# The second half of a feed-forward layer in float16 pairs instead of float32, in a transformer block on one core

## The chip, the core and the metric

The kernel runs on 1 core of a Trainium2 chip. The core has five engines that run their own lists of instructions in order and meet at semaphores: TensorE (PE; matrix products, with PEld for its weight loads), VectorE (DVE), ScalarE (ACT), GpSimd (POOL) and SyncE (SP, which here only starts transfers). The metric is the device time of one execution in microseconds.

## The reference

One transformer block over x of shape (2, 512, 256), in float32: layer norms with per-batch scale, shift and gate computed from a vector c; attention with 32 heads over 8 key-value heads of width 64; and a mixture of experts in LoRA form, of which this case is about the second half.

```
logits = xf @ gate_w.T;  top_w, top_i = top_k(logits, 2);  routing = softmax(top_w)
base1 = xf @ w1.T;       base3 = xf @ w3.T                 # F = 704, E = 8 experts, R = 16
for each expert e with weight we:                          # zero but for the two chosen
    h1 = base1 + xf @ A1.T @ B1.T * 2;   h3 = base3 + xf @ A3.T @ B3.T * 2
    act = silu(h1) * h3
    acc += we * (act @ w2.T + act @ A2.T @ B2.T * 2)
x = x + gb * acc
```

## The kernel before

All arithmetic runs transposed: features on the 128 partitions, the 512 tokens of one batch along the free axis. A float32 product whose operands are split into a float16 high part and a float16 low part is done as three float16 matmuls (`mm3`: high x high, low x high, high x low). Attention and the feed-forward part's first half do that. A high part is a cast on ScalarE (`..._h`), a low part the difference of value and high part, on VectorE or GpSimd (`..._l`).

The attention part runs in 67 periods, n = -3 to 63, one head per period. Each engine's list is written out for the periods: TensorE transposes the probabilities of head n+1, multiplies those of head n with the values, and computes the scores of heads n+2 and n+3; ScalarE casts probabilities and takes exponentials; VectorE takes row maxima, subtracts, and normalises. Weights come in 30 chunks of 256 KB through four staging slots (`wst`), are cast by ScalarE (`w_h`) and differenced by GpSimd (`w_l`). In period 54 SP loads `a2` and `w2` in float32 into the space of used chunks (L340, L341).

The feed-forward part takes the two batches in turn (b = 0, 1), each in FT = 6 tiles of up to 128 of the 704 features (the sixth has 64), i = 6b + f. For each token only the two chosen experts matter. Masks of the routing (`maskT`) let one product serve both. TensorE, for tile f: `h_base` and `h_lora` of tile f+1 (12 + 6 float16 matmuls), `h_second` of tile f (6 more, which add the difference between second and first choice to the same banks), then `z_product`: the a2 product, in float32, of each choice s (L638). ScalarE takes the silu of h1 (`sil`, L888), VectorE multiplies by h3 (`pr`, L1195) and by the routing weight (`av`, L1202), and GpSimd adds both choices (`gsum`, L1363). After the sixth tile TensorE multiplies the sums with w2 and adds the b2 product of the masked LoRA sum `uT`, for four tiles of 128 tokens, in float32 (L700, L704). VectorE multiplies the result by the gate and adds it to x (`store_sum`, L1211, L1214), and SP stores it.

In the first batch's six tiles the three slower engines' lists also hold what the second batch needs: row statistics and norm (L913 to L945), modulation (`hT`, L818, L820), logits, first and second choice (L1110 to L1145), weights, masks (L863) and LoRA inputs (`tm`, L1162, L857, L1166).

What sets the order is the written list of each engine alone. There is no planner.

Of the kernel before, what the change touches and what calls it, by code (L numbers as in the profile page):

```python
# [8 lines left out]
F16 = mybir.dt.float16  # L9
# [35 lines left out]
N_CHUNKS = FFN_CHUNK + FFN_CHUNKS  # L45
WSLOTS = 4
# [51 lines left out]
def block_kernel(nc, x, chunks, cos, sin, cT, wmod, w2T, gateT, a2T, b2T, out, spill):  # L98
    ctx = ExitStack()
    with ctx:  # L100
# [16 lines left out]
        b2_sb = sb("b2_sb", [P, D])  # L117
# [53 lines left out]
        gsum = sb("gsum", [P, FT, S])  # L171
        uT = sb("uT", [P, 2, S])
        maskT1 = sb("maskT1", [P, 5, S])
        tm1 = sb("tm1", [P, 4, S])

# [19 lines left out]
        w2_sb = chunk_space(w_h, 0, [P, FT, D])  # L195
        a2_sb = chunk_space(w_l, 0, [P, FT, P])
# [6 lines left out]
        def ffn_cols(t, at, n):  # L203
# [5 lines left out]
                        for t in (w_h, w_l))  # L209
        maskT = (maskT0, maskT1)  # L210
# [3 lines left out]
        ld_x, ld_x1, ld_c, ld_mod, ld_mod2, ld_rope, ld_ffn, ld_w2 = (  # L214
            sem(f"ld_{k}") for k in ("x", "x1", "c", "mod", "mod2", "rope", "ffn", "w2"))
# [10 lines left out]
        wh_ready, wl_ready = sem("wh_ready"), sem("wl_ready")  # L226

# [17 lines left out]
            "h2h", "h2l", "h_mm", "silu", "p", "a", "g", "d_mm", "z_mm", "zm", "u", "o_mm", "og", "o")}  # L245
# [24 lines left out]
        def _(sp):  # L270
# [43 lines left out]
            sp.dma_start(b2_sb[:, :], b2T).then_inc(ld_ffn, 16)  # L314
# [9 lines left out]
            for n in range(FIRST_PERIOD, HEADS):  # L324
# [27 lines left out]
        def _(pe):  # L352
# [170 lines left out]
            for n in range(FIRST_PERIOD, HEADS):  # L523
# [893 lines left out]
```

## Time and profile before

| | |
|---|---|
| three runs, us | 547.51, 547.8, 545.5; median 547.51 |
| profiled execution: time, span | 547.47 us, 545.5 us |
| mean granted TensorE clock | 0.967 |
| PE busy (share of the span), instructions | 473.2 us (87%), 4424 |
| DVE, ACT, POOL busy | 364.1 (67%), 332.2 (61%), 275.2 us (50%) |
| chain that ended last, by engine | PE 65%, DVE 12%, ACT 11%, issue 7%, DMA 3% |
| L700, w2 product, and L638, a2 product, in that chain | 4%, 3% |

The span is the time between the first and last recorded instruction; the device time is 2.0 us longer. Matmuls are pipelined, so the record of one matmul (0.38 us for 512 float16 columns) is longer than the step to the next. A float32 matmul is recorded as two. In the page's line PEclk, one digit for each fortieth of the span, 9 is full clock; the slices at 450 and at 330 us are lower.

### The profile page before, as it was taken

The numbers are of one execution on the slowest core, as the hardware profiler recorded it, in microseconds if no ns is written. First come the engines' busy times: TensorE is split into PE (matmuls) and PEld (weight loads), VectorE is DVE, ScalarE is ACT, GpSimd is POOL, SyncE is SP. The second block draws the span as 40 slices with busy tenths as digits, with TensorE's granted clock in tenths as the row PEclk, the third lists the DMA queues.
The fourth block names the chain that finished last, engine by engine and source line by source line (L and its number), as shares of the span: only waits on it lengthen the run. The fifth ranks groups of instructions, "written<-read, shape, count | busy, mean of one in ns | idle before, by whom it ended". The sixth has DMA issues, their size and how long they took to land.

```text
span 545.5 us, 11950 instructions
## 1 busy us (share of the span) xinstructions
PE 473.2 (87%) x4424; PEld 324.4 (59%) x4424; DVE 364.1 (67%) x1022; ACT 332.2 (61%) x592; POOL 275.2 (50%) x202
## 2 busy tenths in 40 slices
PE   4777688889999999999999956889788979999997
PEld 3353556576676777777777735667654534464444
DVE  3674866778777778777788868887757766423342
ACT  3336579888878878888888874877624443101110
POOL 4345488885759876669999663310102313101110
PEclk9977889999999999999999996999999989999999
DMA  8046041585333564333545322251110000010001
GB/s 306 31 136 212 21 117 41 155 159 153 99 72 85 157 116 130 106 82 94 174 103 122 89 41 77 59 158 23 30 30 0 2 0 1 0 34 6 0 2 38
DMA packets 58169, 44.47 MB, mean 82 GB/s; under 512 B 36608, under 2 KB 50432, under 8 KB 58112
## 3 DMA queue, kind: packets, MB, share of 16 engines
q1 hardware_dynamic: 56624, 41.60, 29.5%
q10 hardware_dynamic: 1488, 2.10, 1.1%
q8 instruction: 36, 0.59, 0.5%
q14 instruction: 21, 0.17, 0.1%
HBM read 23.77 MB, written 11.53 MB: 65 GB/s over the span
## 4 chain that ended last, share of the span: by engine, by line
PE 65%; DVE 12%; ACT 11%; issue 7%; DMA 3%; POOL 1%; SPq 0%; ACTq 0%; DVEq 0%
PE ps L454 10%; PE ps L380 8%; PE ps L381 8%; PE ps L382 8%; ACT prob L763 6%; PE ps L700 4%; PE ps L472 4%; PE ps L436 4%; PE ps L476 4%; PE ps L438 4%; PE ps L474 4%; PE ps L638 3%; PE ps L628 3%; DVE pl L1044 2%; DMA spill<-rot 1%
## 5 line engine op out<-in xcount | busy, mean ns | idle before, releaser
L763 ACT ACTIVATE prob<-prob,least 128x512 f32<-128x512 f32 (+3 forms) x256 | 131.7, 551 | 3.1 <-DVE least L1036 3.1
L454 PE MATMUL ps<-ident,prob 128*128 128x128 f32 x640 | 95.2, 284 | 35.6 <-DVE pl L1044 19.7
L1036 DVE CUSTOM_DVE_ANT_0 prob<-ps,causal 128x512 f32<-128x512 f32 (+3 forms) x256 | 114.5, 485 | 11.9 <-PE ps L438 11.4
L770 ACT ACTIVATE ph<-ps 128x512 f16<-128x512 f32 (+1 forms) x128 | 89.5, 700 | 43.6 <-PE ps L454 40.1
L454 PEld LDWEIGHTS ps<-ident,prob 128*128 128x128 f32 x640 | 69.4, 143 | 50.5 <-DVE pl L1044 26.0
L1044 DVE SCALAR_TENSOR_TENSOR pl<-ps,ph 128x512 f16<-128x512 f32 (+1 forms) x128 | 99.1, 815 | 0.0
L436 PE MATMUL ps<-kT_h,qT 128*128 128x512 f16 (+3 forms) x256 | 77.3, 303 | 6.7 <-DMA qT<-spill 4.1
L1301 POOL TENSOR_TENSOR on_l<-on,on_h 128x512 f16<-128x512 f32 x32 | 37.1, 1161 | 87.2 <-ACT on_h L777 87.2
L438 PE MATMUL ps<-kT_l,qT 128*128 128x512 f16 (+3 forms) x256 | 70.7, 304 | 0.0
L472 PE MATMUL ps<-vh,ph 128*128 128x65 f16 x640 | 66.9, 197 | 0.6 <-DVE acc L1068 0.6
L474 PE MATMUL ps<-vl,ph 128*128 128x64 f16 x640 | 66.8, 196 | 0.0
L476 PE MATMUL ps<-vh,pl 128*128 128x65 f16 x640 | 66.7, 196 | 0.0
L472 PEld LDWEIGHTS ps<-vh,ph 128*128 128x128 f16 x640 | 60.2, 99 | 1.2 <-DVE pl L1044 0.9
L474 PEld LDWEIGHTS ps<-vl,ph 128*128 128x128 f16 x640 | 60.0, 100 | 0.6
L1053 DVE RECIPROCAL rsum<-ps 128x4 f32<-128x4 f32 x64 | 11.7, 183 | 72.4 <-PE ps L476 72.4
L476 PEld LDWEIGHTS ps<-vh,pl 128*128 128x128 f16 x640 | 59.9, 99 | 0.0
L380 PE MATMUL ps<-hT_h,w_h 128*128 128x512 f16 (+1 forms) x136 | 54.4, 400 | 5.8 <-DVE hT_l L965 2.9
L1363 POOL TENSOR_TENSOR gsum<-av 128x512 f32<-128x512 f32 (+1 forms) x12 | 15.2, 1264 | 86.1 <-DVE av L1202 86.1
L381 PE MATMUL ps<-hT_l,w_h 128*128 128x512 f16 (+1 forms) x136 | 54.4, 400 | 0.0
L382 PE MATMUL ps<-hT_h,w_l 128*128 128x512 f16 (+1 forms) x136 | 53.8, 395 | 0.0
L888 ACT ACTIVATE sil<-ps 128x512 f32<-128x512 f32 (+1 forms) x24 | 13.5, 594 | 65.6 <-PE ps L628 65.5
L1296 POOL TENSOR_TENSOR rot<-rot 128x1024 f16<-128x1024 f32 x19 | 40.6, 2137 | 16.4 <-ACT rot L742 16.3
(150 smaller groups left out, 957.2 us busy)
## 6 DMA issues: line engine op xcount, KB each, us to landing
spill<-rot SPq DMA_DIRECT2D x20, 512.0 KB, 3.6
qT<-spill SPq DMA_DIRECT2D x16, 512.0 KB, 3.5
wst<-chunks SPq DMA_DIRECT2D x30, 256.0 KB, 4.0
kT_h<-spill SPq DMA_DIRECT2D x8, 256.0 KB, 4.0
oT<-wmod ACTq DMA_DIRECT2D x3, 512.0 KB, 11.3
kT_l<-spill SPq DMA_DIRECT2D x4, 256.0 KB, 5.0
out<-xs SPq DMA_DIRECT2D x4, 256.0 KB, 2.1
w_h<-w2T SPq DMA_DIRECT2D x1, 640.0 KB, 5.1
```

What stands on the lines that cost most here:

```text
L380: pe.matmul(o, lh, rh, start=first, stop=False)
L381: pe.matmul(o, lh, rl, start=False, stop=False)
L382: return pe.matmul(o, ll, rh, start=False, stop=last)
L436: pe.matmul(ps[:, bank, off:off + w], qT[:, q_slot(u, j), c], kT_h[:, sg % 2, kv, 0:w], start=True, stop=False)
L438: mm = pe.matmul(ps[:, bank, off:off + w], qT[:, q_slot(u, j), c], kT_l[:, sg % 2, kv, 0:w], start=False, stop=True)
L454: mm = pe.transpose(ps[:, PT_BANK + c // 512, c % 512:c % 512 + P], prob[:, m % 2, c:c + P], ident[:, :])
L472: pe.matmul(ps[:, PV_BANK, at:at + HD + 1], ph[:, m % 2, c:c + P], vh[:, sg % 2, kt, kv, :], start=first, stop=False)
L474: pe.matmul(ps[:, PV_BANK, at:at + HD], ph[:, m % 2, c:c + P], vl[:, sg % 2, kt, kv, :], start=False, stop=False)
L476: mm = pe.matmul(ps[:, PV_BANK, at:at + HD + 1], pl[:, m % 2, c:c + P], vh[:, sg % 2, kt, kv, :], start=False, stop=last)
L763: act.activation(prob[:, m % 2, c], prob[:, m % 2, c], ACT.Exp, bias=least[:, m % 2, qt:qt + 1], scale=-1.0).then_inc(exp_done, 1)
L1036: ins = dve.tensor_tensor_reduce(prob[:, m % 2, at:at + w], ps[:, bank, off:off + w], causal[:, S - w:S], -1.0 / HD ** 0.5, 3.0e38, ALU.ad ...
L1044: dve.scalar_tensor_tensor(out=pl[:, m % 2, c], in0=ps[:, PT_BANK:PT_BANK + 3, :].rearrange("p a b -> p (a b)")[:, c], scalar=PROB_SCALE, ...
```

## The change

The a2, w2 and b2 products become three float16 matmuls each. For that `a2`, `w2` and `b2` are laid out as five more chunks of 256 KB. SP loads all five in period 54 into `raw` and `rot`, buffers of the attention part that are free by then; ScalarE casts one in each of periods 55 to 59, and GpSimd subtracts one in each of periods 56 to 60. The activations `av`, the sums `gsum` and the LoRA sum `uT` are split for each tile. The a2 products of a tile are issued one tile later; those of the sixth tile lie between two pieces of the w2 product; the b2 products of batch 0 come after the first tile of batch 1. The float32 `gsum` keeps two tiles instead of six. The steps that make the second batch's masks and LoRA inputs move one tile later. Cut to its core:

```
@@ kernel constants, SP, ScalarE
+LATE_CHUNKS = LATE_COLS // 512      # 5
+LATE_AT = 54
-                if n == 54:
-                    sp.wait_ge(proj_done, len(TILES))
...
+                if n == LATE_AT:
+                    lowered(sp, len(ITEMS) - 1)
+                    for i in range(LATE_CHUNKS):
+                        sp.dma_start(late_stage(i), chunks[N_CHUNKS + i]).then_inc(ld_late, 16)
+            def late_high(i):
+                act.wait_ge(ld_late, 16 * LATE_CHUNKS)
+                act.wait_ge(proj_done, len(TILES))
+                act.activation(w_h[:, i, :], late_stage(i), ACT.Copy).then_inc(late_h, 1)
@@ TensorE
-            def z_product(b, f, s):
-                pe.wait_ge(fs["a"], 2 * (b * FT + f) + s + 1)
-                mm = pe.matmul(ps[:, 4 + s, :], a2_sb[0:m, f, :], av[0:m, s, :], start=(f == 0), stop=(f == FT - 1))
+            def z_product(b, f):
+                for s in range(2):
+                    pe.wait_ge(fs["al"], 2 * i + s + 1)
+                    mm = mm3(ps[:, 4 + s, :], a2_h[0:m, f, :], a2_l[0:m, f, :], av_h[0:m, i % 2, s, :], av_l[0:m, i % 2, s, :],
+                             f == 0, f == FT - 1)
+            def b2_product(b, t):
+                pe.wait_ge(fs["ul"], b + 1)
+                for l, r in ((u_h, b2_h), (u_h, b2_l), (u_l, b2_h)):
...
                     h_second(b, f)
                     if f > 0:
-                        z_product(b, f - 1, 1)
-                    z_product(b, f, 0)
+                        z_product(b, f - 1)
+                    if b == 1 and f == 0:
+                        for t in range(T):
+                            b2_product(0, t)
...
+                for t in range(2):
+                    for f in range(FT - 1):
+                        w2_product(b, t, f)
+                z_product(b, FT - 1)
+                for t in range(2, T):
+                    for f in range(FT - 1):
+                        w2_product(b, t, f)
+                for t in range(T):
+                    w2_product(b, t, FT - 1)
+            for t in range(T):
+                b2_product(1, t)
@@ ScalarE, each tile
                         act.activation(sil[0:m, s, :], ps[0:m, bank, :], ACT.Silu).then_inc(fs["silu"], 1)
                         if b == 0 and f == 1 and s == 0:
                             modulate_ffn(1, 6)
+                        if i > 0 and s == 0:
+                            sums_high(i - 1)
+                        products_high(i, s)
+                    if b == 1 and f == 0:
+                        lora_sum_high(0)
@@ VectorE, each tile
                     activation_product(b, f, 0)
-                    if b == 1 and f == 0:
-                        store_sum(0)
+                    products_low(b, f, 0)
...
                     activation_product(b, f, 1)
+                    products_low(b, f, 1)
+                    if b == 1 and f == 0:
+                        lora_sum_low(0)
+                    if b == 1 and f == 1:
+                        store_sum(0)
@@ GpSimd, each tile
+                pool.wait_ge(fs["gh"], i + 1)
+                pool.tensor_tensor(gsum_l[0:m, i % FT, :], gsum[0:m, i % 2, :], gsum_h[0:m, i % FT, :], ALU.subtract)\
```

VectorE's list from the end of batch 0 into batch 1's second tile, before:

```order
L1242 TENSOR_TENSOR uT<-ps,maskT 128x512 x2
L1244 TENSOR_TENSOR uT<-uT 128x512
L1195 TENSOR_TENSOR pr<-ps,sil 128x512
L1202 TENSOR_TENSOR av<-pr,maskT 128x512
L1211 TENSOR_TENSOR tm<-ps,gates 128x512
L1214 TENSOR_TENSOR xs<-xs,tm 128x512
```

and now:

```order
L1331 TENSOR_TENSOR uT<-ps,maskT 128x512 x2
L1333 TENSOR_TENSOR uT<-uT 128x512
L1271 TENSOR_TENSOR pr<-ps,sil 128x512
L1277 TENSOR_TENSOR av<-pr,maskT 128x512
L1282 TENSOR_TENSOR av_l<-av,av_h 128x512
L1271 TENSOR_TENSOR pr<-ps,sil 128x512
L1277 TENSOR_TENSOR av<-pr,maskT 128x512
L1282 TENSOR_TENSOR av_l<-av,av_h 128x512
L1287 TENSOR_TENSOR u_l<-uT,u_h 128x512
L1271 TENSOR_TENSOR pr<-ps,sil 128x512
```

Each `av` has got an `av_l` behind it, and `u_l`, the low part of batch 0's LoRA sum, stands behind both choices of batch 1's first tile.

TensorE's list at the end of batch 1's first tile (f = 0), before:

```order
L628 MATMUL ps<-tm_h,w_h 128x512
L628 MATMUL ps<-tm_l,w_h 128x512
L628 MATMUL ps<-tm_h,w_l 128x512
L638 MATMUL ps<-av,w_l 128x512
L380 MATMUL ps<-hT_h,w_h 128x512
```

and now (of the twelve b2 rows, four tiles of tokens, the first three):

```order
L644 MATMUL ps<-tm_h,w_h 128x512
L644 MATMUL ps<-tm_l,w_h 128x512
L644 MATMUL ps<-tm_h,w_l 128x512
L677 MATMUL ps<-w_h,u_h 128x256
L677 MATMUL ps<-w_l,u_h 128x256
L677 MATMUL ps<-w_h,u_l 128x256
```

The tile's a2 product has gone to the next tile, and the b2 products of batch 0 have come from the end of that batch.

## Rows read from the trace of the kernel before

**Rows 1.** Busy time by stage: window, then PE, PEld, DVE, ACT, POOL busy us (count).

```profile
414.00:474.00 60.00, 53.30 (x236) 25.82 (x233) 38.10 (x75) 25.25 (x39) 15.89 (x12) 0.97 0.00 1
...
488.00:527.50 39.50, 38.48 (x150) 16.42 (x148) 16.30 (x25) 6.01 (x11) 7.58 (x6) 1.00 0.02 7
```

**Rows 2.** Waits of 420 to 545 us: total us, times, longest.

```profile
PE ps L628 <- DVE pr L1195: 3.1, 4, 1.2
```

**Rows 3.** Timeline, TensorE: start us, busy us, then the instruction.

```profile
365.60 0.27 PE L381 MATMUL ps<-w_l,oT 128*128 128x256 f16 x1
365.71 0.27 PE L382 MATMUL ps<-w_h,oT 128*128 128x256 f16 x1
...
474.07 3.02 PE L700 MATMUL ps<-w_h,gsum 128*128 128x256 f32 x12 [0.26 <-issue]
...
487.80 0.38 PE L380 MATMUL ps<-hT_h,w_h 128*128 128x512 f16 x1
...
499.19 1.88 PE L638 MATMUL ps<-av,w_l 128*128 128x512 f32 x4
500.91 0.38 PE L380 MATMUL ps<-hT_h,w_h 128*128 128x512 f16 x1
501.12 0.38 PE L381 MATMUL ps<-hT_l,w_h 128*128 128x512 f16 x1
...
540.73 0.70 PE L704 MATMUL ps<-b_sb,uT 128*128 128x256 f32 x2
```

**Rows 4.** One source line each: durations ns min/median/max.

```profile
L857 ACT ACTIVATE tm_h<-tm x8: 629/630/631, 412.0 to 458.7; 128x512 f16<-128x512 f32 x8
...
L965 DVE TENSOR_TENSOR hT_l<-hT,hT_h x2: 693/693/693, 14.5 to 15.8; 128x512 f16<-128x512 f32 x2
...
L1166 DVE TENSOR_TENSOR tm_l<-tm,tm_h x4: 682/1166/1655, 414.3 to 459.1; 128x512 f16<-128x512 f32 x4
...
L1363 POOL TENSOR_TENSOR gsum<-av x12: 1255/1266/1271, 423.7 to 526.2; 128x512 f32<-128x512 f32 x10, 64x512 f32<-64x512 f32 x2
```

**Rows 5.** Timeline, VectorE, first batch of the feed-forward part.

```profile
428.02 0.68 DVE L1195 TENSOR_TENSOR pr<-ps,sil 128x512 f32<-128x512 f32 x1
...
434.68 1.08 DVE L1114 TENSOR_TENSOR fsm<-fsm,rev 128x32 f32<-128x32 f32 x1
...
437.13 0.69 DVE L1195 TENSOR_TENSOR pr<-ps,sil 128x512 f32<-128x512 f32 x1
...
448.78 0.69 DVE L1195 TENSOR_TENSOR pr<-ps,sil 128x512 f32<-128x512 f32 x1 [4.95 <-ACT sil L888]
```

**Rows 6.** Timeline, TensorE and VectorE, from products to `pr`.

```profile
492.77 0.38 PE L628 MATMUL ps<-tm_h,w_l 128*128 128x512 f16 x1
...
493.25 0.69 DVE L1195 TENSOR_TENSOR pr<-ps,sil 128x512 f32<-128x512 f32 x1 [3.83 <-PE ps L628]
...
522.79 0.40 PE L628 MATMUL ps<-tm_h,w_h 128*64 128x512 f16 x1 [0.81 <-DVE pr L1195]
```

**Rows 7.** Timeline, VectorE, its last operation.

```profile
542.20 0.69 DVE L1214 TENSOR_TENSOR xs<-xs,tm 128x512 f32<-128x512 f32 x1
```

**Rows 8.** Timeline, TensorE, after its longest wait in this part.

```profile
445.12 1.09 PE L571 MATMUL ps<-ident,wide 128*128 128x128 f32 x4 [3.18 <-ACT maskT L863]
446.00 0.64 PE L380 MATMUL ps<-hT_h,w_h 128*128 128x512 f16 x1
```

**Rows 9.** Windows of 1 us; PEclk, DMA share and GB/s at the end.

```profile
359.00:360.00 1.00, 1.00 (x27) 0.99 (x26) 0.55 (x4) 0.94 (x2) 0.24 (x1) 1.00 1.02 342
445.00:446.00 1.00, 0.88 (x4) 0.85 (x5) 0.00 (x0) 0.47 (x1) 0.00 (x0) 0.50 0.00 0
```

**Rows 10.** Timeline, ScalarE and TensorE, attention, head 56 to 57.

```profile
362.18 0.49 ACT L763 ACTIVATE prob<-prob,least 128x256 f32<-128x256 f32 x1
...
362.96 0.88 PE L454 MATMUL ps<-ident,prob 128*128 128x128 f32 x6 [0.21 <-DVE pl L1044]
```

**Rows 11.** Transfers: how often, KB each, us from issue to landing.

```profile
w_h<-w2T SPq DMA_DIRECT2D x1, 640.0 KB, 5.1
```

More of the change, by code:

```diff
@@ L170, in block_kernel @@
         tm_h, tm_l = (sb(f"tm_{k}", [P, B, 4, S], F16) for k in "hl")
-        gsum = sb("gsum", [P, FT, S])
+        gsum_h, gsum_l = (sb(f"gsum_{k}", [P, FT, S], F16) for k in "hl")
+        gsum = sb("gsum", [P, 2, S])
         uT = sb("uT", [P, 2, S])
@@ L174, in block_kernel @@
         tm1 = sb("tm1", [P, 4, S])
+        av_h, av_l = (sb(f"av_{k}", [P, 2, 2, S], F16) for k in "hl")
+        u_h, u_l = (sb(f"u_{k}", [P, S], F16) for k in "hl")
         def over(t, shape):
@@ L694, in _ @@
                     pe.wait_ge(fs["og"], 2)
-                for i in range(2):
-                    for t in range(2 * i, 2 * i + 2):
-                        at = (t % 2) * D
-                        for f in range(FT):
-                            m = min(P, F - f * P)
-                            pe.matmul(ps[:, 6 + i, at:at + D], gsum[0:m, f, t * P:(t + 1) * P], w2_sb[0:m, f, :],
-                                      start=(f == 0), stop=False)
-                        if t == 0:
-                            pe.wait_ge(fs["u"], b + 1)
-                        mm = pe.matmul(ps[:, 6 + i, at:at + D], uT[:, 1, t * P:(t + 1) * P], b2_sb[:, :],
-                                       start=False, stop=True)
-                    mm.then_inc(fs["o_mm"], 1)
+                for t in range(2):
[9 more added lines that the diff above has]
+                b2_product(1, t)
         @block.scalar
@@ L874, in weights_wide, with products_high, sums_high, lora_sum_high @@
                        .then_inc(fs[name], 1)
+            def products_high(i, s):
+                m = min(P, F - i % FT * P)
+                act.wait_ge(fs["a"], 2 * i + s + 1)
+                wait(act, fs["z_mm"], 2 * i + s - 3)
+                act.activation(av_h[0:m, i % 2, s, :], av[0:m, s, :], ACT.Copy).then_inc(fs["ah"], 1)
+            def sums_high(i):
+                m = min(P, F - i % FT * P)
+                act.wait_ge(fs["g"], i + 1)
+                if i == FT:
+                    act.wait_ge(fs["w2_mm"], T)
+                act.activation(gsum_h[0:m, i % FT, :], gsum[0:m, i % 2, :], ACT.Copy).then_inc(fs["gh"], 1)
+            def lora_sum_high(b):
+                act.wait_ge(fs["u"], b + 1)
+                if b > 0:
+                    act.wait_ge(fs["o_mm"], 2)
+                act.activation(u_h[:, :], uT[:, 1, :], ACT.Copy).then_inc(fs["uh"], 1)
             weights_wide(0)
@@ L1196, in activation_product @@
                 dve.wait_ge(fs["p"], q + 1)
-                wait(dve, fs["z_mm"], q - 1)
                 if i > 0:
@@ L1202, in activation_product, with products_low, lora_sum_low @@
                 dve.tensor_tensor(av[0:m, s, :], pr[0:m, s, :], maskT[b][0:m, 3 + s, :], ALU.mult).then_inc(fs["a"], 1)
+            def products_low(b, f, s):
+                m, i = min(P, F - f * P), b * FT + f
+                dve.wait_ge(fs["ah"], 2 * i + s + 1)
+                dve.tensor_tensor(av_l[0:m, i % 2, s, :], av[0:m, s, :], av_h[0:m, i % 2, s, :], ALU.subtract)\
+                   .then_inc(fs["al"], 1)
+            def lora_sum_low(b):
+                dve.wait_ge(fs["uh"], b + 1)
+                dve.tensor_tensor(u_l[:, :], uT[:, 1, :], u_h[:, :], ALU.subtract).then_inc(fs["ul"], 1)
             def store_sum(b):
```

111 lines of the change are left out of this document (72 added, 39 removed).

## The prediction

> **What bounds the kernel now.** I read the busy table by stage first, then the waits of the feed-forward part, then TensorE's and VectorE's rows in order of time. The table by stage [rows 1] says that from 414 us on TensorE is what is full: 53.3 of 60 us for the first batch's tiles, 38.5 of 39.5 us for the second's. The reader is to see beside it how little the others do in the second batch (VectorE 16.3, ScalarE 6.0, GpSimd 7.6 us of 39.5). The waits say the same: TensorE's products waited for VectorE's `pr` 3.1 us in all, in four places [rows 2]. So an edit that takes time from TensorE gains, as long as the work that it puts on VectorE, ScalarE and GpSimd does not become the later end. That is the question of this case, and it is decided tile by tile, since each engine runs its list in order.
>
> **Term 1, TensorE's own work.** Before, one float32 product of 512 columns took two records: four records from 499.19 to 500.91 us are two products, so 0.86 us each [rows 3]. Three float16 products take 3 x 0.2155 = 0.65 us (the step from one to the next, 500.91 to 501.12 [rows 3]). The a2 product occurs 24 times: 24 x 0.215 = -5.2 us. The w2 and b2 products of one batch ran from 474.07 to 487.80 [rows 3], 13.7 us for 28 products, 3.43 us for each of four row tiles. With 256 float16 columns the step is 0.109 us [rows 3], so 21 matmuls make 2.29 us. 8 x 1.14 = -9.1 us. Together -14.3 us, if TensorE never waits more than before.
>
> **Term 2, what the three other engines get.** Each tile now has, for both choices, a ScalarE cast of `av` and a VectorE subtraction, and for the sum a cast and a GpSimd subtraction. The prices: a cast to float16 0.63 us (`tm_h`); the same subtraction on VectorE 0.69 us where GpSimd is still, and 1.17 us median, up to 1.66, where GpSimd runs beside it (`tm_l`); `gsum` 1.27 us [rows 4]. `gsum` starts exactly when the second `av` ends, so it overlaps the second subtraction; I take 0.7 for the first and 1.1 for the second. The Trainium skill (GPSIMD Engine Reference, Specifications) says that GpSimd's SBUF interfaces are shared with VectorE, with contention for VectorE instructions that have two SBUF inputs. By that rule the new subtractions suffer and `pr`, which reads PSUM, does not; the spread of `tm_l` from 0.68 to 1.66 us agrees. Without the rule every chain below would be 0.4 us shorter and the sum some 1.5 us less.
> The added work is in a chain. VectorE's list for one choice is `pr`, `av`, wait for ScalarE's cast, `av_l`: 0.73 + 0.72 + 0.66 + 0.72 = 2.8 us, twice per tile 5.7 us, 6.1 with the contention. TensorE's tile is 30 matmuls = 6.47 us. So in steady state TensorE still sets the pace, with some 0.4 us to spare, and every extra item on VectorE's list now shows.
>
> **Term 2a, batch 0.** VectorE's list there also holds the second batch's norm, choices and masks. I walk from `pr` to `pr` with the durations above. Tile 0: the first subtraction comes ahead of the second `pr` (+0.5), cast and subtraction ahead of the row statistics (+0.66 and +1.1): `pr` of tile 1 moves from 428.02 [rows 5] to about 430.3. Tile 1: ScalarE casts `gsum` and `av` (1.25) behind the four `hT` copies and ahead of the second silu, then come cast and subtraction again; part is won back, because the first choice's small operations already waited for GpSimd (one took 1.08 us) and now start when it is nearly through: `pr` of tile 2 from 437.13 [rows 5] to 441.0. Tile 2: one subtraction ahead of the second choice, cast and subtraction ahead of the weights: `pr` of tile 3 from 448.78 [rows 5] to 453.6. From there the masks, moved a tile later, and the added casts keep the distance; TensorE reaches w2 at 479.1 instead of 474.07, behind the last mask copy. Up to here TensorE's saving (10 a2 products, 2.2 us, and two put behind) is spent in idling. Then w2 without b2 and with one tile's a2 pair: 60 + 12 matmuls x 0.109 + 6 x 0.2155 = 9.1 us against 13.7. Second batch starts at 488.25 against 487.80: +0.45.
>
> **Term 2b, batch 1.** The new wait: after tile 0's second products TensorE issues b2 for batch 0, and that needs `u_l`. On VectorE `u_l` stands behind `pr`, `av` and `av_l` of tile 0's second choice, and this `pr` needs the very matmuls that TensorE has just issued. The row of before gives the start: last of these matmuls issued at 492.77 (the next could go at 492.99), `pr` at 493.25 [rows 6], 0.27 us behind. Sum: 0.27 + 0.73 + 0.72 + 0.66 + 0.72 (1.1 beside `gsum`) + 0.72 = 3.8 to 4.2 us in which TensorE has nothing. All of tile 1's 30 matmuls are queued behind it. I take +4.0. Then the 12 b2 matmuls, moved here from batch 0, 1.3 us. Tile 2: the store's four operations (4 x 0.71) stand ahead of its first `pr`; from the end of tile 1's products 0.27 + 0.73 + 0.72 + 0.66 + 0.9 + 2.85 + 0.7 = 6.8 us, against z and 18 matmuls, 5.2 us: +1.7. Tiles 3 and 4 keep up. Tile 5 has no base matmuls ahead: between its two neighbours TensorE has 1.3 us of a2 while VectorE needs 4.0: +2.7, where before 0.81 us of waiting stood [rows 6], and 1 us more in the last a2 products. Adding TensorE's list: 5 x 3.9 (base and LoRA) + 6 x 1.29 + 6 x 1.29 + 8.4 (waits) + 1.3 + 7.9 (w2) + 1.3 (b2) = 54.1 us, against 487.80 to 541.4 [rows 3], 53.6 us: +0.45. Last, both halves of the output come 0.65 us apart and the multiply-add pairs stand in line: last store's input at 544.7 us, before 542.89 [rows 7]. Sum of terms 1 and 2: **+1.8 us**.
>
> **Term 3, the clock.** A wait of 3.18 us at 442 us brought the granted clock to 0.5 of full, which is 1.2 GHz, and the next matmuls took 0.64 us each instead of 0.38 [rows 8, 9]; full clock was back some 3 us after the wait had ended, 1.5 us lost. The 4.0 us wait is longer than that one, so it pays the 1.5 in full; those of 2.7 and 2.8 us are between. In batch 0 TensorE idles anyway behind it. Bounds 0 and 4.5; I take +2.0.
>
> **Term 4, the weights' way.** SP now issues five 256 KB loads where a2 and w2 (1.06 MB) stood, behind one `qT` fetch of 512 KB: 1.84 MB in all. The transfers of this place ran at 342 GB/s from 359 on [rows 9], and w2's 640 KB landed 5.1 us after their issue [rows 11]. 1.84 MB at 342 GB/s take 5.4 us, from about 358 to 363.4. ScalarE comes to the first cast at 362.18, in front of the `prob` exponential that TensorE's transposes at 362.96 need [rows 10]: it waits for all five. The transposes of the last tile, due at 363.5, get it 0.6 + 0.5 us after landing, at 364.4 or later. Bounds 0 (landed by 362.2) and 2.5 (365); I take +1.0. The other four casts (0.6 us each) lie beside TensorE's transposes and value products, and GpSimd's five beside nearly nothing of its own: 0; if that cover is gone, 0.5 us each, 2.0. The b2 load taken from the start (128 KB) lay behind all that anyone waited for: 0.
>
> Sum: 547.47 + 1.8 + 2.0 + 1.0 = **552.3 us**. The profiled execution (547.47) is that of the median (547.51).
>
> **Rivals.** R1, faster: the casts and subtractions disappear in idle time, of which ScalarE has 33 of 39.5 us and VectorE 23 [rows 1], and TensorE sets the end: 547.5 - 14.3 = 533, or somewhat above it. For it speaks the table; against it, that idle time of an engine with its list in order isn't free time, and the 4.0 us chain has no other way round. It decides from added waits under 11.6 us in all; I count 16.1 (1.8 + 14.3), terms 3 and 4 not in it. R2, no change: mechanism as forecast, but neither clock nor landing cost anything: 549.3. For it: only one wait surely exceeds the 3.18 us. R3, much slower: the clock falls in each of four waits (+4.5), loads land at 365 (+2.5), and the subtractions take 1.17 us everywhere, which takes VectorE's tile to 6.6 us, above TensorE's 6.47, and lengthens each chain by 0.4 (+2): 547.5 + 1.8 + 9 = 558. Against R2 stands the Trainium skill (TensorE: Matmul & The Clock Gate, What's actually happening): the throttled state is the default and activity releases it. By it a long wait costs twice, once idle and once slow; the trace at 445 us agrees.
>
> **Numbers.** Forecast 0.47, R1 0.13, R2 0.25, R3 0.15. 0.5% is 2.7 us, about what can be told from none: faster means under 544.8, slower over 550.3. R1 is faster, R2 within, forecast and R3 slower: 0.13, 0.25, 0.62. The range takes in R2 and most of R3's way: 545 to 557; the forecast's own is 550 to 555.
>
> **What would show it.** TensorE idle about 4 us in batch 1 before the first b2 matmul, with a release by `u_l`; matmuls of 0.64 us behind it; w2 of batch 0 starting near 479 plus term 4; a2 in steps of 0.2155; ScalarE waiting for a DMA at 362 for 1 to 2 us. Wrong if TensorE's wait at b2 is under 2 us, or if batch 0 reaches w2 before 476.

## The result, and the profile after

The changed kernel takes 564.22 us (median of 4 runs, 560.98 to 565.22) against 546.50 beside it (4 runs, 545.33 to 547.80): ratio 1.031, 95% interval 1.028 to 1.034. That is slower by 17.7 us. I had forecast 552.3, and it lies outside my range of 545 to 557. The profiled execution took 565.22 us, its span 563.3; before, 547.47 and 545.5.

The page of after, busy time of each engine and the granted clock in 40 slices:

```profile
PE 468.9 (83%) x4504; PEld 321.9 (57%) x4504; DVE 391.0 (69%) x1048; ACT 356.4 (63%) x635; POOL 295.8 (53%) x219
...
PEclk9977889999999999999999969989799988998989
```

TensorE is busy 468.9 us of 563.3, only 4.3 less than before, and VectorE has moved up from 364.1 to 391.0. The busy time hides part of TensorE's saving, since at half clock the record of 512 float16 columns is 0.63 us long and not 0.38. In steps the products cost what I had counted (term 1 below), yet the kernel is longer: idle time and slow clock ate more than was saved. The table by stage answers to [rows 1] (window, its length, then PE, PEld, DVE, ACT, POOL busy; the last three numbers are granted clock, DMA share and GB/s):

```profile
420.00:489.60 69.60, 52.11 (x246) 24.85 (x243) 50.61 (x87) 34.64 (x57) 22.48 (x17) 0.95 0.00 1
489.60:499.20 9.60, 9.57 (x78) 7.23 (x78) 4.25 (x7) 1.61 (x3) 1.15 (x1) 1.00 0.01 2
499.20:547.60 48.40, 39.32 (x170) 17.00 (x170) 29.53 (x37) 15.80 (x28) 12.56 (x11) 0.93 0.03 11
```

The first row is batch 0's tiles, the second its w2 products, the third batch 1's tiles. In batch 1 TensorE was idle 9.1 us of 48.4, where before it was 1.0 of 39.5, and VectorE is busy 29.5 us where it had been 16.3. In the waits of 420 to 563 us (total, times, longest), the row that answers to [rows 2] has gone from 3.1 to 12.7 us, and there is a new one above it, VectorE waiting for ScalarE's casts:

```profile
DVE av_l L1282 <- ACT av_h L927: 18.9, 24, 3.0
...
PE ps L644 <- DVE pr L1271: 12.7, 6, 2.9
```

The stages are laid out by four marks: ScalarE's last `on_h` (end of attention), VectorE's first `pr`, TensorE's first w2 product of batch 0, and the end of the span. From `on_h` to the first `pr` it is 21.2 us in all kernels. Each row is one profiled execution. (e1 to e12 are the experiments of the next section.)

| kernel | last on_h | first pr to w2 | w2 to end | span |
|---|---|---|---|---|
| before | 398.65 | 54.17 | 71.43 | 545.5 |
| after | 405.07 | 63.32 | 73.67 | 563.3 |
| e1 late casts | 396.07 | 63.35 | 74.33 | 555.0 |
| e2 before + late loads | 403.18 | 54.20 | 71.40 | 550.0 |
| e3 b2 a tile later | 403.91 | 63.37 | 70.19 | 558.7 |
| e4 subtractions last | 405.92 | 61.85 | 76.00 | 565.0 |
| e5 no av_l | 404.86 | 58.26 | 69.26 | 553.6 |
| e6 no gsum_l | 403.30 | 59.41 | 72.97 | 556.9 |
| e7 skewed | 404.34 | 59.07 | 71.36 | 556.0 |
| e8 w2 half only | 397.68 | 55.20 | 66.09 | 540.2 |
| e9 all moved | 398.63 | 59.51 | 67.24 | 546.6 |
| e10 two moves | 398.61 | 62.95 | 70.22 | 553.0 |
| e11 av_l on GpSimd | 396.57 | 58.10 | 66.10 | 542.0 |
| e12 the same, batch 0 | 399.15 | 58.09 | 65.64 | 544.1 |

After against before: attention +6.4, tiles of batch 0 +9.15, the rest +2.2, 17.8 us in all.

**Attention.** SP's and ScalarE's rows where the late loads stand, to be read with [rows 10, 11]:

```profile
358.87 0.44 SPq L357 DMA_DIRECT2D rot<-chunks  x1
...
365.18 0.63 ACT L781 ACTIVATE w_h<-raw 128x512 f16<-128x512 f32 x1 [2.86 <-DMA rot<-chunks]
```

The fifth load was issued at 358.87 and landed about 365.1, 6.3 us later, and ScalarE stood in its DMA wait for 2.86 us. TensorE's wait for the exponential behind it, and the transfers and the clock around it (the first window is 359 to 363 us):

```profile
366.26 0.65 PE L470 MATMUL ps<-ident,prob 128*128 128x128 f32 x2 [2.60 <-ACT prob L807]
```

```profile
359.00:363.00 4.00, 3.37 (x48) 2.31 (x45) 3.06 (x11) 3.27 (x6) 0.88 (x2) 1.00 0.99 355
363.00:365.00 2.00, 0.66 (x4) 0.42 (x4) 1.25 (x6) 0.00 (x0) 0.56 (x1) 1.00 0.19 62
366.00:370.00 4.00, 3.43 (x39) 2.74 (x40) 1.37 (x5) 3.74 (x8) 1.28 (x2) 0.57 0.16 33
```

TensorE's next products start 3.0 us late by this wait, and then they run at a granted clock of 0.57 where before it was 1.00 from 360 to 374. The 30 value products of one head take 1.67 us instead of 0.91. From there every head is 4.0 us late, 3.0 by the wait and 1.0 by the clock, and that is never made up. The end of attention, and the clock there:

```profile
405.07 0.63 ACT L821 ACTIVATE on_h<-on 128x512 f16<-128x512 f32 x1 [7.09 <-DVE on L1133]
```

```profile
400.00:405.00 5.00, 3.75 (x41) 2.68 (x39) 1.86 (x6) 0.00 (x0) 0.00 (x0) 0.61 0.13 26
510.00:520.00 10.00, 10.00 (x41) 4.28 (x40) 3.02 (x5) 2.45 (x5) 1.28 (x1) 0.84 0.00 0
```

`on_h` waited 7.09 us where before it was 4.69, and at 400 to 405 us the granted clock is 0.61 where it had been 1.00: 2.4 us more. The second window (510 to 520 us) belongs to batch 1, below.

**Batch 0**, VectorE's `pr` of tiles 1, 2 and 3, answering to [rows 5], and one `av` that stands beside GpSimd's new `gsum_l`:

```profile
436.70 0.68 DVE L1271 TENSOR_TENSOR pr<-ps,sil 128x512 f32<-128x512 f32 x1
...
449.06 0.69 DVE L1271 TENSOR_TENSOR pr<-ps,sil 128x512 f32<-128x512 f32 x1
...
461.56 0.69 DVE L1271 TENSOR_TENSOR pr<-ps,sil 128x512 f32<-128x512 f32 x1 [2.98 <-ACT sil L956]
...
462.28 1.54 DVE L1277 TENSOR_TENSOR av<-pr,maskT 128x512 f32<-128x512 f32 x1
```

Counted from tile 0's `pr` (419.90 before, 426.31 after) they are 2.3, 5.5 and 6.4 us late. TensorE then reached w2 at 489.63, 9.2 us late by the same count, behind the last mask:

```profile
489.63 0.28 PE L667 MATMUL ps<-w_h,gsum_h 128*128 128x256 f16 x1 [0.41 <-ACT maskT L909]
```

**Batch 1.** The wait that b2 adds, answering to [rows 6], from tile 0's second `pr` to TensorE's first b2 product:

```profile
504.67 0.69 DVE L1271 TENSOR_TENSOR pr<-ps,sil 128x512 f32<-128x512 f32 x1 [6.02 <-PE ps L644]
505.39 0.69 DVE L1277 TENSOR_TENSOR av<-pr,maskT 128x512 f32<-128x512 f32 x1
506.12 0.63 ACT L927 ACTIVATE av_h<-av 128x512 f16<-128x512 f32 x1 [1.57 <-DVE av L1277]
...
506.78 1.20 DVE L1282 TENSOR_TENSOR av_l<-av,av_h 128x512 f16<-128x512 f32 x1 [0.70 <-ACT av_h L927]
...
507.90 0.68 DVE L1287 TENSOR_TENSOR u_l<-uT,u_h 128x512 f16<-128x512 f32 x1
...
508.64 0.28 PE L677 MATMUL ps<-w_h,u_h 128*128 128x256 f16 x1 [4.08 <-DVE u_l L1287]
```

It is 4.08 us. The list is as I had counted it: `pr`, `av`, the cast, `av_l` stretched to 1.20 by `gsum` beside it, then `u_l`. Behind the store of batch 0 VectorE goes at this pace (one tile, from tile 3's first `pr` to tile 4's first):

```profile
529.49 0.68 DVE L1271 TENSOR_TENSOR pr<-ps,sil 128x512 f32<-128x512 f32 x1
530.20 1.26 DVE L1277 TENSOR_TENSOR av<-pr,maskT 128x512 f32<-128x512 f32 x1
532.16 0.69 DVE L1282 TENSOR_TENSOR av_l<-av,av_h 128x512 f16<-128x512 f32 x1 [0.70 <-ACT av_h L927]
532.77 0.68 DVE L1271 TENSOR_TENSOR pr<-ps,sil 128x512 f32<-128x512 f32 x1
533.49 0.69 DVE L1277 TENSOR_TENSOR av<-pr,maskT 128x512 f32<-128x512 f32 x1
534.87 1.21 DVE L1282 TENSOR_TENSOR av_l<-av,av_h 128x512 f16<-128x512 f32 x1 [0.69 <-ACT av_h L927]
536.00 0.68 DVE L1271 TENSOR_TENSOR pr<-ps,sil 128x512 f32<-128x512 f32 x1
```

Two `pr` 0.68, two `av` 0.69 and 1.26, two waits for the cast 0.70, two `av_l` 0.69 and 1.21: 6.51 us from `pr` to `pr`, where TensorE's list takes 6.47. TensorE waits for `pr` in tile 2 and in front of tile 5, and not in between:

```profile
524.29 0.39 PE L644 MATMUL ps<-tm_h,w_h 128*128 128x512 f16 x1 [2.13 <-DVE pr L1271]
...
543.23 0.40 PE L644 MATMUL ps<-tm_h,w_h 128*64 128x512 f16 x1 [2.88 <-DVE pr L1271]
```

### The profile page after: what moved, and what is told of

The parts are those of the page before. It is cut to its first block, busy times and chain, and to the rows that moved or that the text cites. A ratio compares the mean times of both kernels' runs of the same rounds, so it can differ in the third digit from the quotient of the medians.

```text
span 563.3 us, 12223 instructions
## 1 busy us (share of the span) xinstructions
PE 468.9 (83%) x4504; PEld 321.9 (57%) x4504; DVE 391.0 (69%) x1048; ACT 356.4 (63%) x635; POOL 295.8 (53%) x219
## 4 chain that ended last, share of the span: by engine, by line
PE 54%; DVE 17%; ACT 13%; issue 8%; DMA 4%; POOL 2%; SPq 1%; ACTq 0%; DVEq 0%
PE ps L470 10%; PE ps L396 7%; PE ps L397 7%; PE ps L398 7%; ACT prob L807 6%; PE ps L488 4%; PE ps L492 4%; PE ps L490 3%; PE ps L452 3%; PE ps L454 3%; PE ps L667 3%; DVE av L1277 3%; DVE pr L1271 2%; DVE pl L1120 2%; ACT av_h L927 2%
## 5 line engine op out<-in xcount | busy, mean ns | idle before, releaser
L488 PE MATMUL ps<-vh,ph 128*128 128x65 f16 x640 | 68.6, 199 | 0.6 <-DVE acc L1144 0.6
L490 PE MATMUL ps<-vl,ph 128*128 128x64 f16 x640 | 68.6, 197 | 0.0
L492 PE MATMUL ps<-vh,pl 128*128 128x65 f16 x640 | 68.5, 197 | 0.0
L396 PE MATMUL ps<-hT_h,w_h 128*128 128x512 f16 (+1 forms) x136 | 55.9, 411 | 10.3 <-DVE pr L1271 4.7
L397 PE MATMUL ps<-hT_l,w_h 128*128 128x512 f16 (+1 forms) x136 | 55.7, 409 | 0.0
L398 PE MATMUL ps<-hT_h,w_l 128*128 128x512 f16 (+1 forms) x136 | 55.1, 405 | 0.0
L1390 POOL TENSOR_TENSOR rot<-rot 128x1024 f16<-128x1024 f32 x19 | 40.6, 2135 | 16.3 <-ACT rot L786 16.3
L1360 POOL TENSOR_TENSOR w_l<-wst,w_h 128x512 f16<-128x512 f32 x30 | 34.9, 1165 | 26.9 <-ACT w_h L776 26.9
```

The lines of the kernel that those rows point to most:

```text
L396: pe.matmul(o, lh, rh, start=first, stop=False)
L397: pe.matmul(o, lh, rl, start=False, stop=False)
L398: return pe.matmul(o, ll, rh, start=False, stop=last)
L488: pe.matmul(ps[:, PV_BANK, at:at + HD + 1], ph[:, m % 2, c:c + P], vh[:, sg % 2, kt, kv, :], start=first, stop=False)
L490: pe.matmul(ps[:, PV_BANK, at:at + HD], ph[:, m % 2, c:c + P], vl[:, sg % 2, kt, kv, :], start=False, stop=False)
L492: mm = pe.matmul(ps[:, PV_BANK, at:at + HD + 1], pl[:, m % 2, c:c + P], vh[:, sg % 2, kt, kv, :], start=False, stop=last)
```

## The experiments

All twelve kernels are the changed kernel with one thing altered, unless it says otherwise. e5 and e6 leave out part of the arithmetic, so their results differ; they serve for their times alone. Ratios are to the kernel before, with their 95% interval.

**e1, casts two periods later.**

```diff
-                if LATE_AT < n <= LATE_AT + LATE_CHUNKS:
-                    late_high(n - LATE_AT - 1)
+                if LATE_AT + 2 < n <= LATE_AT + 2 + LATE_CHUNKS:
+                    late_high(n - LATE_AT - 3)
```

GpSimd's `late_low` is moved by the same two periods.

> The changed kernel with ScalarE's five late casts in periods 57 to 61 instead of 55 to 59 and GpSimd's subtractions in 58 to 62; the loads stay where they are. Landing theory (ScalarE stands 2.86 us in a DMA wait at 362.2, every head after it is 4.0 us late, and the clock at the end of attention takes 2.4 more): no DMA wait on ScalarE, attention's last on_h at 399 to 401 instead of 405.07, total 557.5 to 560.5. Rival (the loss belongs to the casts and subtractions themselves, which displace exponentials, or to the loads' traffic on the queues): last on_h still at 404 or later, total 562.5 to 564.5. If only the landing wait goes and the clock's fall stays: 560.

Measured 557.05 us, 1.0191 (1.0161 to 1.0221), 7 us better than the changed kernel and 0.5 us below the range of the landing theory. ScalarE's first cast and its last `on_h`:

```profile
369.00 0.62 ACT L781 ACTIVATE w_h<-raw 128x512 f16<-128x512 f32 x1
...
396.07 0.63 ACT L821 ACTIVATE on_h<-on 128x512 f16<-128x512 f32 x1 [4.69 <-DVE on L1133]
```

No DMA wait is left, and the last `on_h` waits 4.69 us as before. (This execution was 2.6 us early long before the loads: at 60 to 80 us its granted clock was 0.98 where the kernel before had 0.85. Taking that off, attention ends where it ended before, 398.65; in e9 and e10 it does so to 0.04 us.) So five casts and five subtractions, with their loads, cost attention nothing if nobody waits for the landing. The feed-forward part is that of the changed kernel, with 63.35 us in batch 0.

**e2, the loads alone in the kernel before.** Five `chunks` loads at period 54, casts and subtractions as in the change, written to weight chunks 6 to 9 and 12; the a2 and w2 loads at period 60.

> The kernel before with one part of the change: the five late loads, casts and subtractions at the same periods, into weight chunks that are free by then and that nobody reads; the loads of a2 and w2 move six periods on. The feed-forward part is that of before. Landing theory: attention's last on_h goes from 398.65 to about 405 (6.4 us), total 551.5 to 553.5. Rival (the six us of attention come from elsewhere in the change): 546.5 to 548.5. Whatever it costs is the part of the 17.9 us that my term 4 had put at 1.0.

Measured 552.52, 1.0111 (1.0081 to 1.0142). The same two rows:

```profile
365.66 0.63 ACT L757 ACTIVATE w_h<-raw 128x512 f16<-128x512 f32 x1 [2.66 <-DMA rot<-chunks]
...
403.18 0.63 ACT L797 ACTIVATE on_h<-on 128x512 f16<-128x512 f32 x1 [4.69 <-DVE on L1079]
```

The wait is there, 2.66 us, and attention ends 4.5 us late. Of these the execution had 0.7 already before the wait (its `on_h` ahead of it stands at 362.38, before at 361.66), so that the wait and what follows it cost 3.8 us. (By the medians e2 is 6.3 us longer than the kernel before. The profiled execution of e2 is its fastest; that of the kernel before lies 1.3 us above the median beside e2.) At the end the last `on_h` waits only 4.69 us: the clock did not fall there.

Seven profiles have ScalarE waiting for the landing (after, e2 to e7), 2.66 to 3.55 us. Directly behind the wait the clock falls in all seven, to 0.78 to 0.87 over 360 to 370 us; in the seven without the wait it is 1.00 there. Counted from the `on_h` ahead of the wait, this part costs 3.8 to 4.3 us in six of them. It costs 6.0 in e3, where the wait is longest and the clock stays at 0.50 from 366 to 372. At the end of attention four of the seven show an `on_h` wait of 7.05 to 7.09 us and a clock of 0.54 to 0.78 between 395 and 405 us (after, e4, e5, e7), 2.4 us more, and three show neither; of the seven without the landing wait none does. What decides that second fall was not found.

**e3, b2 and the store one tile later.**

```diff
-                    if b == 1 and f == 0:
+                    if b == 1 and f == 1:
                         for t in range(T):
                             b2_product(0, t)
...
-                    if b == 1 and f == 1:
+                    if b == 1 and f == 2:
                         store_sum(0)
```

> The changed kernel with the b2 products of batch 0 one tile later (behind tile 1's second products and tile 0's a2) and the store of batch 0 one tile later too. Wait theory: TensorE's 4.08 us wait for u_l goes, and with it the clock's fall to 0.84 in 510 to 520, total 558.5 to 560. Rival (VectorE's own list of 6.5 us a tile sets the end of batch 1, so that a wait of TensorE ahead of it is no loss): VectorE still has 10 tile halves of 3.26 us and the store's 3.3 us behind the first tile, the wait turns up again in front of its first product, total 562.5 to 564.5.

Measured 561.06, 1.0247 (1.0187 to 1.0307): between the two theories by the median, since its runs spread from 556.45 to 562.03. The stages are clearer: batch 0 the same to 0.05 us, w2 to end 70.19 instead of 73.67, so the two moves were worth 3.5 us. TensorE has no wait for `u_l`. `pr` of tile 1 comes at 507.39 and 510.33, where after had 508.50 and 517.09 (e3 reached w2 1.1 us earlier). The wait theory holds and the rival falls, though VectorE keeps its 6.5 us a tile from there on. The b2 products and the store were moved together; what each gives alone was not run.

**e4, both subtractions of a tile behind its second product.**

```diff
-                    products_low(b, f, 0)
                     if b == 0 and f == 2:
                         second_choice(1)
                     activation_product(b, f, 1)
+                    products_low(b, f, 0)
                     products_low(b, f, 1)
```

> The changed kernel with VectorE's two subtractions of a tile behind its second product instead of one behind each product; the same instructions, only their order. Pace theory (VectorE's tile is 6.51 us: 4 products 3.3 to 3.9, two subtractions 1.9, and two waits of 0.70 for ScalarE's cast, against TensorE's 6.47, so that no lateness is ever made up): both waits vanish from VectorE's list, its tile is 5.1 to 5.7 us, the 3.3 us of the store and most of the lateness of batch 0 are made up, TensorE's waits for pr of 2.88 and 2.13 us fall under 1.5, total 555 to 559. Rival (contention with GpSimd and the falls of the clock are what costs, the order on VectorE does not): 562 to 565.

Measured 565.52, 1.0330 (1.0275 to 1.0385): no gain, and my pace theory in this form is wrong. A tile of batch 1, VectorE and ScalarE:

```profile
530.89 0.68 DVE L1271 TENSOR_TENSOR pr<-ps,sil 128x512 f32<-128x512 f32 x1
...
532.89 0.63 ACT L927 ACTIVATE av_h<-av 128x512 f16<-128x512 f32 x1 [1.81 <-DVE av L1277]
...
533.43 0.58 ACT L956 ACTIVATE sil<-ps 128x512 f32<-128x512 f32 x1
...
534.04 0.69 DVE L1271 TENSOR_TENSOR pr<-ps,sil 128x512 f32<-128x512 f32 x1 [1.18 <-ACT sil L956]
...
535.37 2.36 DVE L1282 TENSOR_TENSOR av_l<-av,av_h 128x512 f16<-128x512 f32 x2
...
537.66 0.68 DVE L1271 TENSOR_TENSOR pr<-ps,sil 128x512 f32<-128x512 f32 x1
```

VectorE's waits for the cast are gone, as I had wanted, but 1.18 us for ScalarE's silu has come in their place. ScalarE's list has the cast `av_h` ahead of the next silu, the cast waits for `av`, and `pr` waits for the silu. The way from `av` to the next `pr` went through ScalarE all along; the subtraction only hid it. And both subtractions, now side by side with GpSimd's `gsum`, took 1.18 us each. The tile is 6.77 us.

**e5, without the subtractions of av_l** (the a2 products read `av_h` twice).

> The changed kernel without VectorE's 24 subtractions that make av_l; the a2 products read av_h in place of av_l (24 products with other operands, the same number and size). ScalarE's casts stay. What e4 left standing: ScalarE's next silu stands behind the cast of the product before it, 1.18 us from the end of av to the next pr; the subtraction adds 0.7 to 1.2 us behind that cast. Pace theory: VectorE's tile falls from 6.51 us to 2 x (0.68 + 0.69 to 1.26 + 1.18) = 5.1 to 6.2, under TensorE's 6.47, so that the store's 3.3 us and part of batch 0's lateness are made up, and the wait for u_l is 1.4 us shorter: 555 to 558.5. Rival (ScalarE's casts alone keep the pace): 561 to 564.

Measured 555.78, 1.0160 (1.0112 to 1.0208). Both stages shrink, by 5.1 and 4.4 us, and `pr` waits for the silu as in e4:

```profile
521.51 0.69 DVE L1271 TENSOR_TENSOR pr<-ps,sil 128x512 f32<-128x512 f32 x1 [1.18 <-ACT sil L956]
```

From 518.91 it is 2.60 us a half, 5.2 a tile, under TensorE's 6.47. So 24 subtractions of 0.7 to 1.2 us were worth 8 to 9 us of the end.

**e6, without the subtractions of gsum_l** (the third w2 product reads `gsum_h`).

> The changed kernel without GpSimd's 12 subtractions that make gsum_l; the third w2 product reads gsum_h instead. Contention theory (GpSimd's subtraction lies beside VectorE's av and stretches it from 0.69 to 1.26 us, once a tile): that av takes 0.69, VectorE's tile is 5.9 us, total 559 to 562. Rival (the wait for the cast absorbs it, or the stretch moves to another operation): tile at 6.5, total 563 to 565.

Measured 559.48, 1.0245 (1.0200 to 1.0291), as the contention theory said. Three `pr`, one tile:

```profile
517.27 0.68 DVE L1271 TENSOR_TENSOR pr<-ps,sil 128x512 f32<-128x512 f32 x1
...
519.99 0.68 DVE L1271 TENSOR_TENSOR pr<-ps,sil 128x512 f32<-128x512 f32 x1
...
523.22 0.68 DVE L1271 TENSOR_TENSOR pr<-ps,sil 128x512 f32<-128x512 f32 x1
```

2.72 and 3.23 us, a tile of 5.95: the `av` that took 1.26 us beside `gsum_l` takes 0.69. The half that has `gsum` beside its `av_l` is unchanged. In the changed kernel no engine shows a wait for `gsum_l`, so it cost by what it did to its neighbour, and that was 3.9 us in batch 0.

**e7, cast and subtraction one product later, on both engines.**

```diff
                     activation_product(b, f, 0)
-                    products_low(b, f, 0)
+                    if f > 0:
+                        products_low(b, f - 1, 1)
...
                     activation_product(b, f, 1)
-                    products_low(b, f, 1)
+                    products_low(b, f, 0)
+                    if f == FT - 1:
+                        products_low(b, f, 1)
```

On ScalarE likewise: silu of a product first, then the cast of the product before it.

> The changed kernel with cast and subtraction of each product one product later: ScalarE does silu q and then the cast of q-1 (the cast of the sums behind it), VectorE pr q, av q and then the subtraction of q-1. The same instructions. Queue theory (from e4: both the wait for the cast on VectorE and the silu that stands behind the cast on ScalarE lie between av and the next pr, so the order has to change on both engines at once): neither wait is left, VectorE's tile is 2 x (0.68 + 0.69 to 1.26 + 0.69 to 1.2) = 4.1 to 6.3, near 5.5, total 555 to 559. Rival (order doesn't matter, VectorE beside GpSimd and the clock do): 562 to 565, as in e4.

Measured 556.91, 1.0184 (1.0136 to 1.0233): 7 us with the same instructions. VectorE's tile in batch 1:

```profile
520.98 0.69 DVE L1276 TENSOR_TENSOR pr<-ps,sil 128x512 f32<-128x512 f32 x1 [0.30 <-PE ps L644]
521.71 1.45 DVE L1282 TENSOR_TENSOR av<-pr,maskT 128x512 f32<-128x512 f32 x1
...
523.69 0.68 DVE L1276 TENSOR_TENSOR pr<-ps,sil 128x512 f32<-128x512 f32 x1
524.99 0.69 DVE L1282 TENSOR_TENSOR av<-pr,maskT 128x512 f32<-128x512 f32 x1 [0.63 <-POOL gsum L1470]
...
527.46 0.69 DVE L1276 TENSOR_TENSOR pr<-ps,sil 128x512 f32<-128x512 f32 x1 [1.17 <-PE ps L644]
```

No wait for a cast, none for a silu: VectorE waits 0.63 us for GpSimd's `gsum` and 1.17 us for TensorE, and the tile is 6.48 us, TensorE's own. The `av` beside `gsum_l` even takes 1.45 us; where VectorE has slack that costs nothing. e4 and e7 tell it apart from a count of instructions: the new order on VectorE alone gave nothing, on both engines at once it gave 7 us. ScalarE's order alone was not run.

**e8, only the w2 half.** Sums and LoRA sum in float16 pairs; a2, its activations and its products in float32 as before, `av` in two buffers; late casts and b2 place as in e1 and e3.

> Half of the change: sums and LoRA sum in float16 pairs, a2 and its products in float32 as before (the products in two buffers where av_h and av_l lay, a2 loaded in period 60), with the late casts of e1 and the b2 place of e3. Theory (the av casts and subtractions cost more than the 5.2 us that they save TensorE, the w2 half pays): VectorE's list is nearly that of the kernel before, TensorE saves 8 x 1.14 = 9.1 us, total 537 to 542, below before. Rival (the w2 half with the store's move and GpSimd's subtraction costs as much as it saves, too): 545 to 549.

Measured 543.09, 0.9925 (0.9897 to 0.9953): faster than before, by 4 us, and 1 us above the upper end of what I had put. TensorE's wait for `pr` (total, times, longest):

```profile
PE ps L649 <- DVE pr L1268: 7.3, 6, 2.1
```

Batch 0 costs 1.0 us more than before and w2 to end 5.3 less. It is the fastest kernel of the study.

**e9, all three moves on the whole change** (e1, e3 and e7); **e10, e1 and e3 without e7.**

> The whole change with three moves and nothing left out: casts two periods later (e1), b2 and the store one tile later (e3), cast and subtraction of each product one product later on ScalarE and VectorE (e7). If the three losses are separate, their gains add: against the changed kernel 7.2 + 3.2 + 7.4 us, total 545 to 548, even with the kernel before. TensorE theory (with nothing but TensorE left to set the end, the saving of 14.3 us appears): 533 to 538. Against e8 (543.1): below it if the a2 half pays once its chain is hidden, above it if VectorE still holds TensorE up.

> The changed kernel with the late casts of e1 and the b2 place of e3, but each subtraction behind its own product as in the changed kernel. Pace theory: VectorE's 6.5 us a tile stay, so what e3 gains is only the 4 us wait: 557 - 3.2 = 552.5 to 555.5. The difference to e9 is the price of the order on ScalarE and VectorE by itself, 6 to 8 us. Rival (in e7 the gain came from the clock): the two are within 3 us.

e9 measured 548.32, 0.9999 (0.9977 to 1.0021), e10 554.32, 1.0131 (1.0108 to 1.0153). The three losses are largely separate: together the moves gain 15.9 us, one by one 7.2, 3.2 and 7.3, which is 17.7. e9 is 0.3 us above the range I had put, and the order on ScalarE and VectorE is worth 6 us by itself. The TensorE theory (533 to 538) did not come true. By stage e9 wins 4.2 us behind w2 and loses 5.3 in batch 0. TensorE's waits for `pr` in batch 0 (410 to 480 us) and two windows of it:

```profile
PE ps L644 <- DVE pr L1276: 6.4, 3, 3.0
```

```profile
430.00:440.00 10.00, 8.27 (x35) 4.83 (x34) 6.37 (x12) 5.02 (x9) 5.03 (x4) 0.72 0.00 0
450.00:460.00 10.00, 7.29 (x25) 3.64 (x26) 4.10 (x6) 4.89 (x9) 2.81 (x2) 0.66 0.00 0
```

The granted clock is 0.72 and 0.66 in stretches in which TensorE waits; in the kernel before one stretch of 10 us in batch 0 had 0.83, the others 1.00.

**e11, e9 with the subtractions of av_l on GpSimd; e12, in batch 0 only.**

> e9 with all 24 subtractions that make av_l on GpSimd instead of VectorE. e9 lies 1.1 us of span over the kernel before, and 5.3 of it between the first pr and the first w2 product of batch 0, where VectorE also has the second batch's statistics, choices and masks. Load theory (VectorE's list in batch 0 is what holds TensorE up): GpSimd's tile is 1.3 + 3 x 1.2 = 4.9 us, under 6.47, VectorE is free of 12 x 0.7 to 1.2 us in batch 0; first pr to first w2 falls from 59.5 to 56 to 58, total 543 to 546. Rival (contention: each GpSimd operation of 1.2 us stretches the VectorE operation beside it by 0.5, and av waits for GpSimd's subtraction before it may overwrite): 548 to 553.

> As e11, but only in batch 0; in batch 1 VectorE makes av_l as in e9. Load theory: the same gain in batch 0 as e11, batch 1 as in e9, total 543 to 546. If contention costs more than the list frees, batch 0 of e11 and of this kernel are both longer than 59.5 us, and this one lies between e9 and e11: 548 to 550.

e11 measured 545.72, 0.9984 (0.9957 to 1.0010), e12 545.47, 0.9975 (0.9948 to 1.0001). Batch 0 takes 58.1 us in both instead of 59.5: the load theory holds, but for 1.4 us only, at the short end of what I had put (56 to 58). Contention takes back part of what VectorE's list was freed of: the median `av` of batch 0 is 1.32 us in e11 and 0.76 in e9. Behind w2 both are shorter than e9 too, by 1.1 and 1.6 us. e12 has e9's order there, but e9's execution had a clock of 0.83 at 520 to 530 where e11's and e12's had 1.00. The other 3.9 us over the kernel before in batch 0 stay open: casts on ScalarE, the masks moved a tile later and the clock are what is left, and none was tried by itself. The clock has the size for it. What the windows of 10 us from 410 to 480 fell short of full clock adds up to 1.7 us in the kernel before, 6.8 in e9 and 5.1 in e11 and e12, so 5.1 and 3.4 us more, where the stage lost 5.3 and 3.9. But the clock fell where TensorE had waited, and part of that time it would have waited anyway, so this is a measure and not a cause shown.

## Why the prediction was wrong

The mechanisms were nearly all named. Direction and places were right, the sizes were not. The kernel took 17.8 us more of span where I had summed 4.8. Of the 13.0 between, 5.4 lie in attention (term 4), 4.2 in batch 0 (term 2a) and 3.4 behind it (terms 2b and 3).

**Bound and Term 1** (TensorE, -14.3 us): right as a sum of work. a2 goes in steps of 0.216, w2 in steps of 0.109 us, and batch 0's w2 stretch with its a2 pair took 9.6 us where I had 9.1. As a gain it never appears whole: in the best kernel with the whole change (e12) the stage from w2 to the end is 5.8 us shorter.

**Term 4** (the weights' way, +1.0, bounds 0 and 2.5): the largest single miss, 6.4 us measured. The step that failed is "1.84 MB at 342 GB/s take 5.4 us, from about 358 to 363.4" taken as the landing. The rate held: 355 GB/s from 359 to 363, and 62 from 363 to 365. But ScalarE was released at 365.1, 1.7 us after the time in my sum. The trace of before had shown as much, in a row that I had passed over for the 5.1 us of the piece ahead of it. This is w2's last piece, issued at 358.61 and so landed at 365.3:

```profile
w_h<-w2T SPq DMA_DIRECT2D x1, 64.0 KB, 6.7
```

My upper bound of 365 had the wait about right, 2.86 us, but I priced the delay as if the wait were the whole of it. The heads come 4.0 us late, 3.0 by TensorE's wait and 1.0 by the clock behind it, and e2 gives 3.8 for this alone. By their lists ScalarE's exponentials, TensorE's transposes and the copies behind them form one ring per head, and no head made the lateness up. The other 2.4 us are the second fall of the clock, at the end of attention. Term 3 had neither fall.

**Term 2a** (batch 0, w2 +5.0): +2.3 for tile 1 as predicted, then +5.5 for 3.9, +6.4 for 4.8, and +9.2 for 5.0 at w2. The step "from there the masks and the added casts keep the distance" failed: another 2.8 us were lost in tiles 4 and 5. I had left `gsum_l` out of VectorE's durations altogether; e6 gives it 3.9 us of this stage. The trace had shown both prices [rows 4], and e6 agrees with the rule I had cited (the Trainium skill, GPSIMD Engine Reference, Specifications: VectorE's instructions with two SBUF inputs contend with GpSimd); I had used it for the pair `gsum` and `av_l` and not for `gsum_l` and `av`.

**Term 2b** (batch 1): the waits were right, 4.08, 2.13 and 2.88 us for 4.0, 1.7 and 2.7, and e3 gives the first 3.5 us of the end. "Tiles 3 and 4 keep up" was right too: TensorE has no wait in them. "VectorE 5.7 us, 6.1 with the contention, 0.4 us to spare" failed: its tile is 6.51, with 0.57 us of that same `av` in it, against TensorE's 6.47. So VectorE has nothing to spare, and what it is late by behind the store it does not make up. The tiles of batch 1 took 48.4 us; my list, without the b2 and w2 products at the end and the last a2 pair, gave 43.4. Of the 5.0 between, 0.7 are waits, 3.3 the clock in the windows 510 to 520 and 540 to 550, and the rest small gaps. The sum in the prediction had slips as well: its terms add up to 53.9 and not 54.1, and the "1 us more in the last a2 products" stands in none of them.

**Term 3** (clock, +2.0, bounds 0 and 4.5): right in kind, and too small where I had put it. Behind the waits of batch 1 the windows 510 to 520 and 540 to 550 show 0.84 and 0.83, 3.3 us. Three windows of 10 us in batch 0 have 0.83, 0.94 and 0.89, 3.4 us in part while TensorE waited, where the kernel before had 1.7. With the 1.0 and 2.4 us of attention, for which the term had nothing, it is up to 8.4 us more than before.

**The rivals.** R3 (558) had the mechanisms: VectorE's tile over 6.47, the loads at 365, the clock in several waits. I had given it 0.15, and its price was short by 6 us. R1's claim, that idle engines hide the casts, is what e7, e9 and e12 build by hand; with all of it the kernel is even with the one before, not at 533.

What the twelve runs settle: about 6.4 of 17.8 us is the wait for the landing and its clock, 3.5 the wait for `u_l` with the store's place, 6 to 7 the order of cast, silu and subtraction. The 3.9 us that e6 gives `gsum_l` in batch 0 can be in part the same us as these; e6 and e7 were not run together. The changed kernel without the three (e9) is at 0.9999, so the 14.3 us that TensorE was to save still do not show. Behind w2 it gains 4.2, and batch 0 loses 5.3, for which no run shows the cause.

## What to carry to other kernels

Count for the engine that gets the added work not only its operations, but the whole ring from its output back to its next input, through each engine's list; here a cast in front of the next silu was that ring, and moving it behind, with the subtraction, gave 6 us with the same instructions. A list that takes as long as the bound's (here 6.51 us against 6.47) makes up no delay. A landing is to be read from the last load of the place before, not from bytes over a rate. And of a change in several parts ask which pays alone. The w2 half (9.1 us of TensorE for 12 casts and 12 subtractions, on engines that wait anyway) did: e8 is 0.9925. The a2 half (5.2 us for 24 casts and 24 subtractions in the ring) did not: with it the kernel is at 0.9999 (e9) and at best 0.9975 (e12).

## What the runs showed of the hardware

- Contention goes by pairs. VectorE's 512-column subtraction or product with both inputs in SBUF took 0.69 us alone, 1.20 beside GpSimd's sum of two float32, and 1.26 to 1.54 beside GpSimd's subtraction with a float16 result; GpSimd's `gsum` itself rose from 1.27 to 1.65 us when it had VectorE's two subtractions beside it (e4). `pr`, with one input in PSUM, stayed at 0.67 to 0.69 in all 24, also where GpSimd's `gsum_l` ran beside it.
- Five loads of 256 KB behind a fetch of 512 KB: the last landed 6.3 us after its issue, though the transfers ran at 355 GB/s from 359 to 363 and at 62 from 363 to 365. In the kernel before a piece of 64 KB at the same place took 6.7 us.
- TensorE's granted clock fell directly behind a landing wait of 2.66 to 3.55 us in all seven executions that had one. At the end of attention, some 35 us later, it fell to 0.54 to 0.78 in four of the seven and not in the other three. The changed kernel's runs of 560.98 and 565.22 us may differ by this; the first was not profiled.
